# A two-layer block of SSM, attention, FWHT-FFN and MoE on one core: attention's statistics at the start of the second mixture pass, head work one block earlier, another order of the stack writes and loads

## The reference, cut to what matters

```python
# mixture (before and after attention), added with a factor 0.5
scores = sigmoid(xt @ gate_w.T); top-2 of 8 experts, weights scaled by 2.5
h = einsum('td,edh->eth', xt, w1); u = einsum('td,edh->eth', xt, w3)     # H = 176
y = einsum('eth,ehd->etd', silu(h) * u, w2)
routed = einsum('etd,te->td', y, combine); shared = silu(xt @ sw1) * (xt @ sw3) @ sw2
# attention, 16 heads of 16, causal, with ALiBi
q, k, v = proj(Wq, bq), proj(Wk, bk), proj(Wv, bv)
scores = q k^T / sqrt(16), masked above the diagonal, + alibi_bias
out = softmax(scores) @ v, then @ Wo.T + bo
```

## Time and profile before

| | us |
|---|---|
| median of 3 runs | 806.44 |
| lowest and highest | 806.35, 807.98 |
| the profiled execution | 805.94 |
| its span in the trace | 804.1 |

### The profile page before, as it was taken

How to read it: one execution, slowest core, us unless ns; L and a number is a source line. 1 busy time by engine, 2 the same in 40 slices (tenths; PEclk the granted TensorE clock), 3 DMA queues, 4 the chain that set the end, 5 groups by cost and what they waited for, 6 DMA issues and landing times.

```text
span 804.1 us, 10910 instructions
## 1 busy us (share of the span) xinstructions
PE 708.6 (88%) x4054; PEld 485.6 (60%) x4089; DVE 549.1 (68%) x962; ACT 405.6 (50%) x594; POOL 242.8 (30%) x190
## 2 busy tenths in 40 slices
PE   3899998895688799899999999994889998788998
PEld 3587664451234354557877887882447887434787
DVE  4544589999979999974457466366755656944644
ACT  3454597676557688742233344450476442274322
POOL 0001158786429587850996000001000001000000
PEclk9999999997999799999999999998999999899999
DMA  8300012222112221318001000043000043000000
GB/s 290 127 2 0 1 66 78 70 77 66 52 39 68 66 73 61 90 42 243 0 1 23 1 1 1 13 107 104 15 1 1 15 121 99 5 28 1 1 1 26
DMA packets 30609, 41.78 MB, mean 52 GB/s; under 512 B 3769, under 2 KB 19971, under 8 KB 30531
## 3 DMA queue, kind: packets, MB, share of 16 engines
q1 hardware_dynamic: 29306, 40.91, 16.9%
q10 hardware_dynamic: 1252, 0.19, 0.2%
HBM read 36.73 MB, written 4.26 MB: 51 GB/s over the span
## 4 chain that ended last, share of the span: by engine, by line
PE 52%; issue 16%; DVE 15%; ACT 6%; DMA 6%; POOL 3%; SPq 2%; POOLq 0%; DVEq 0%; ACTq 0%
PE PS L500 32%; DVE PS L2066 4%; PE PS L607 3%; DVE shared L2074 3%; PE PS L1095 3%; POOL shared L2390 3%; PE PS L1078 2%; DMA route<-scratch_c 2%; ACT shared L1618 2%; DVE route L2124 1%; PE PS L458 1%; DMA scratch_k<-shared 1%; DMA shared<-in_L_ffn_W_dram 1%; SPq L2336 1%; ACT shared L1544 1%
## 5 line engine op out<-in xcount | busy, mean ns | idle before, releaser
L2390 POOL TENSOR_TENSOR shared<-shared,route 128x1024 f32<-128x1024 f32 x64 | 150.6, 2357 | 72.2 <-DVE shared L2074 67.5
L2074 DVE TENSOR_TENSOR_SCAN shared<-shared,PS 128x512 f32<-128x512 f32 x128 | 148.8, 1204 | 2.4 <-ACT shared L1544 1.7
L500 PE MATMUL PS<-xnT,work_r 128*128 128x512 f32 (+1 forms) x596 | 149.8, 398 | 0.4 <-DVE gated L1798 0.2
L500 PE MATMUL PS<-xnT,weights_r 128*128 128x256 f32 (+1 forms) x732 | 147.1, 349 | 1.4 <-issue 1.1
L500 PEld LDWEIGHTS PS<-xnT,weights_r 128*128 128x128 f32 x732 | 113.5, 191 | 47.3 <-issue 33.4
L500 PEld LDWEIGHTS PS<-xnT,work_r 128*128 128x128 f32 (+1 forms) x596 | 109.2, 188 | 25.0 <-DVE gated L1798 1.7
L1544 ACT ACTIVATE shared<-shared,cols 128x512 f32<-128x512 f32 x128 | 85.2, 715 | 28.3 <-DVE shared L2074 27.8
L500 PE MATMUL PS<-weights_r,work_r 128*128 128x256 f32 (+1 forms) x624 | 89.3, 294 | 0.6 <-DVE gated L1923 0.3
L2066 DVE TENSOR_TENSOR PS<-shared,PS 128x512 f32<-128x512 f32 x128 | 81.3, 681 | 3.5 <-PE PS L940 3.1
L500 PEld LDWEIGHTS PS<-weights_r,work_r 128*128 128x128 f32 (+1 forms) x624 | 80.5, 190 | 2.3 <-issue 0.4
L888 PE MATMUL PS<-shared,cf 64*64 64x512 f32 x512 | 75.0, 658 | 0.6 <-POOL shared L2390 0.6
(11 more groups left out here) (231 smaller groups left out, 1052.4 us busy)
## 6 DMA issues: line engine op xcount, KB each, us to landing
route<-scratch_c SPq DMA_DIRECT2D x64, 256.0 KB, 3.2
shared<-in_L_ffn_W_dram SPq DMA_DIRECT2D x3, 1024.0 KB, 8.7
scratch_k<-shared SPq DMA_DIRECT2D x12, 128.0 KB
scratch_q<-shared SPq DMA_DIRECT2D x12, 128.0 KB
shared<-scratch_k SPq DMA_DIRECT2D x8, 192.0 KB
shared<-scratch_q SPq DMA_DIRECT2D x8, 192.0 KB
mamba_w<-in_L_ffn_w_dram SPq DMA_DIRECT2D x2, 704.0 KB, 5.3
beside<-in_L_ffn_w_dram SPq DMA_DIRECT2D x2, 704.0 KB, 7.7
```

The lines of the kernel that those rows point to most:

```text
L500: last = nc.tensor.matmul(o, lhs[l], rhs[r], start=(start and i == 0), stop=(stop and i == 2))
L2074: v.tensor_tensor_scan(hst[:, (t % 2 * 2 + j) * T:(t % 2 * 2 + j + 1) * T], decay[t % D_SLOTS][:, j * T:(j + 1) * T], products[:, j * T:(j ...
L2390: nc.gpsimd.tensor_tensor(hc[:, u * 2 * T:(u * 2 + n) * T].rearrange("p (c t) -> p c t", c=n), hst[:, (t % 2) * 2 * T:(t % 2 * 2 + n) * T] ...
```

## The change

Three things are edited.

- `LATE_NORM_AT` goes from 4 to 3 and `LATE_HEAD_AT` from 6 to 5. Statistics' square root, scaling, transposes, projections, values and casts of the first batch's attention each come one block earlier.
- DVE's `norm_statistics(0)` is taken out of block `LATE_NORM_AT` and stands at the very beginning of the late pass, ahead of the routing.
- SP's order in `attention_moves`, in both batches, was: six writes of c = 0, fill 1, fill 2, six writes of c = 1, fill 3, fill 4. It is now: six writes of c = 0, four of c = 1 (hi and mid), fill 1, the last two writes of c = 1, fill 2, fill 3, fill 4.

```diff
-LATE_NORM_AT, LATE_HEAD_AT, EARLY_CAST_AT = 4, 6, 4
+LATE_NORM_AT, LATE_HEAD_AT, EARLY_CAST_AT = 3, 5, 4
...
+                if late:
+                    self.norm_statistics(0)
                 if early:
                     self.norm(0, it + 1)
...
-                    if late and p == LATE_NORM_AT:
-                        self.norm_statistics(0)
                     if late and p == LATE_NORM_AT + 1:
                         self.norm_scale(0, 2 * ATTN + 1)
...
-                for c in range(DC):
-                    for quad in (2 * c, 2 * c + 1):
-                        sp.wait_ge(s[f"stacked{quad}"], b * 16 * 6)
-                    for i, part in enumerate(("hi", "mid", "lo")):
-                        for n, parts, scratch, _ in sources:
-                            sp.wait_ge(s["cast"], cast_at(b, c, f"{n}_{part}"))
-                            sp.dma_start(scratch[c, i].rearrange("d h t -> h d t"), part_of(parts, c, i))\
-                                .then_inc(s[f"wrote{n}{c}"], 16)
+                def write(c, i):
+
+                    for n, parts, scratch, _ in sources:
+                        sp.wait_ge(s["cast"], cast_at(b, c, f"{n}_{('hi', 'mid', 'lo')[i]}"))
+                        sp.dma_start(scratch[c, i].rearrange("d h t -> h d t"), part_of(parts, c, i))\
+                            .then_inc(s[f"wrote{n}{c}"], 16)
+
+                def fill(c, quad):
...
+                for quad in range(2 * DC):
+                    sp.wait_ge(s[f"stacked{quad}"], b * 16 * 6)
+                for i in range(3):
+                    write(0, i)
+                for i in range(2):
+                    write(1, i)
+                fill(0, 0)
+                write(1, 2)
+                fill(0, 1)
+                fill(1, 0)
+                fill(1, 1)
```

31 lines of the change are left out of this document (15 added, 16 removed).

## The result

| | before | after |
|---|---|---|
| median, us | 806.50 (4 runs, 806.35 to 807.98) | 799.79 (4 runs, 798.86 to 801.02) |
| ratio | | 0.9914, 95% interval 0.9895 to 0.9932 |
| the profiled execution | 805.94 | 799.49 |
| its span | 804.1 | 797.7 |

The kernel is faster by 6.7 us on the medians and by 6.45 us in the profiled executions. The same kernel was run again beside the experiments; over all its 17 executions the median is 799.28.

The account below looks back on a forecast made before the run. PE's 8.8 us wait for fill 3 before the first attention's `late_unit(0)` was taken as the bound. 805.94 - 5.3 (pass's +1.3 included) + 0.5 + 0.2 = 801.3; the median 0.5 above, 801.8 us, range 800.6 to 804.9.

Parts of the forecast that it names:

- The bound: First attention: PE idle 8.8 us before `late_unit(0)`, waiting for fill 3; DVE is what is late next.
- Part 1: Late pass: head work one block earlier makes the pass end 1.3 us later, casts move 3.2 us earlier.
- Part 2: Start of the late pass: statistics cost DVE 2.1 us, hidden in its 2.54 us wait, so nothing.
- Part 3: First batch, SP's new order: fill 3 lands in time, `late_unit(0)` moves from 562.13 to 556.8, -5.3 us.
- The term behind U: First attention, from `late_unit(0)` on: +0.2 us for the queue and +0.5 us for the clock.
- The queue: `scores(0)` waits for the row of maxima behind fill 4's traffic: +0.2 us (0 to 0.6).
- The clock: First attention after `late_unit(0)` will look like the second, wholly or in part: +0.5 us (0 to 1.0).
- Part 4: Second batch, SP's new order: only the fills move, with cover of 5 and 3 us; costs nothing.
- (a): DMA takes the wait over: a further fill costs 9.5 us, `scores(0)` follows no sooner than 566.3; 804.4 us, chance 0.15.
- (d): Slower: more fills in a row drag on each other (F, time per further fill), both batches; 811.8 us, chance 0.07.
- (b): The clock falls in block 4 of the late pass, 2 us lost; 803.8 us, chance 0.09.
- (e): Better: no clock loss and shorter stalls in block 4, -6 us; 800.4 us, chance 0.05.

Follow-up runs that it names:

- e2: Kernel after with SP's old order, so head work one block earlier and statistics at the start alone; 805.06 us, ratio 0.9978.
- e6: Kernel before with only the statistics moved to the start of the late pass; 806.72 us, ratio 1.0003.
- e15: Kernel before with idle products ahead of `late_unit(0)` (26 in the first attention, nine in the second) and four ahead of `scores(4)`; 804.36 us, ratio 0.9973.
- e5: Kernel after, unchanged, run again; 801.47 us, ratio 0.9933.
- e11: Kernel after, unchanged, run a third time; 798.74 us, ratio 0.9905.
- e10: Kernel after with POOL's add of the output bias started so that it always meets DVE's low parts; 800.57 us, ratio 0.9929.
- e9: Kernel after with POOL's add of the output bias held until DVE has taken four maxima; 800.59 us, ratio 0.9928.
- e14: Kernel after with nine idle products ahead of `late_unit(0)` and four ahead of `scores(4)`, in both attentions; 799.42 us, ratio 0.9909.
- e8: Kernel before with 16-row loads of q, nine idle products ahead of `late_unit(0)` and statistics at the start of the late pass; 796.47 us, ratio 0.9885.
- e4: Kernel after with nine idle products ahead of `late_unit(0)` in both attentions; 799.86 us, ratio 0.9913.
- e7: Kernel before with 16-row loads of q and nine idle products ahead of `late_unit(0)`; 797.04 us, ratio 0.9888.
- e12: e8 with POOL's add of the output bias held until DVE has taken four maxima; 797.83 us, ratio 0.9891.
- e13: e8 with four more idle products ahead of `scores(4)` in each attention; 796.51 us, ratio 0.9877.
- e1: Kernel before with SP's new order alone; 803.55 us, ratio 0.9954.
- e3: Kernel before with each broadcast load of q cut into loads of 16 rows; 799.89 us, ratio 0.9908.

## Why the prediction was off

Point by point, in the order of its steps.

- **The bound** was read right: the wait was for fill 3, fill 3 was late by SP's order and ACT's casts, and taking it away leaves DVE.
- **Part 1** came true almost to the tenth. xn was expected at 492.1, and PE's first transposes are at 492.38 after 1.69 us (1.9 expected); the second at 495.38 after 0.73 (495.2, 0.9). R to Q is 1.32 us longer (+1.3).
- **Part 2** came true: DVE's idle 2.54 us became 0.34.
- **Part 3, the fills.** Fill 1 was issued at 528.59 (528.3). Fill 2 landed 20.8 us later and not 19.0: a pair of writes between two fills costs 2.9 us, not 1.1. PE waited 0.51 us for it, which was to be none, but DVE had no gap. Fill 3 was there in time. U: 556.95 against 556.8.
- **The term behind U is the step that failed.** The prediction put +0.2 for the queue and +0.5 for the clock, neither of which could fall below nothing; the measured stretch is 1.18 us shorter. All of it lies between U and `scores(0)`, 6.33 us before and 5.16 after; from there to O both take 31.9. The two profiles split it.
- *The queue, +0.2 put, -1.04 measured.* In the kernel before, `scores(0)` waited 1.04 us for the row of maxima behind fill 4; after, it doesn't wait. The sum's own figures left room for that: the queue was to end 4.8 to 7.4 us earlier than the 568.46 at which the row landed, and PE's start was to move by 5.3. The experiments bear it out. With SP's old order and broadcast loads the stretch takes 6.31 to 6.40 us in before, e2, e6 and e15, whatever the clock (0.51 in e15, 0.76 in before, and e15 still waits 0.16 us). With the new order and at least a part of it at the full level it takes 4.91 to 5.50.
- *The clock, +0.5 put, -0.13 measured.* Without the wait for the row the stretch takes 5.29 us before and 5.16 after. It was written that the first attention "will now look like the second", and lose clock by it. But the earlier trace rows show the first attention of before at 0.50 up to U and at 0.76 behind it: it was already paying, and with a wait of 2.20 us in place of 8.80 it could as well pay less. The second attention's 0.53 was taken for what a wait of 2.20 us brings; it was one draw of several. Behind the same 2.20 us the kernel after took 37.06, 38.07 and 37.05 us from U to O in three profiles, and 39.16, 37.70 and 37.06 in the second attention.
- So part of the 1.18 us is luck. With the draw of e5 (0.50 all the way, 6.06 us, PE itself being late) the end of the queue brings 0.27 us and no more, and the kernel after would have been 0.9 us longer there, still on the side of a gain. Both are needed for the 1.18: a queue that ends in time, and a clock that doesn't stay at the half level all the way.
- **A term was missing.** The prediction went through PE, DVE, ACT and SP, and not through POOL, whose add was freed 11 us earlier by the new writes. It costs 1.6 to 1.75 us from R to Q in the profiles in which it meets DVE's low parts (e5, e11 and, by force, e10). It was absent from the profiled execution, so it isn't in the 5.27, and it works against the change.
- **Part 4** came true: no wait for a stack in the second attention, and U2 waits 2.20 us for DVE as before.
- **The rivals.** None of (a) to (d) came; for (b), the granted clock was 1.00 from 490 to 500. (e), "no clock loss", had the right sign and 800.4, and its reason was half right; it had a chance of 0.05 and stood outside what the range took in. The range's lower end was the forecast's terms at their best, and no term could be below nothing for the clock. With as much room below nothing as above it (-1.0 to +1.0) it would have begun at 799.6, and held the time. (In (d), the balance of the two attentions turns near F = 10.15 by the prediction's own terms, not 10.3; nothing hangs on it.)

What stays open is the median to less than 1 us. e9 and e10 both lie 1.8 us above e11 and differ from it only in POOL's add, whose place explains neither. The mean granted clock of their executions is 0.9673 and 0.9705, and 0.9730 in e11; by the line in the last section that would be some 2.3 and 1.0 us. It isn't shown whether the hold brings that lower clock or whether it was drawn. And e14, with the half level gone from both attentions, isn't faster by its median than after. The last section shows the draws that such medians of five or six executions carry.

## What to carry to other kernels

A clock, a queue or a wait that the profile shows as already paid is a term that can be given back: ask of each whether it is paid now before adding it to the change's price, and leave it room on both sides of nothing. When a transfer moves up, follow its semaphore to every engine that waits on it, the idle ones too; work that was harmless where it stood can land beside an instruction that it stops. And before work is rearranged around a slow transfer, look at how many DMA engines share it: here 16-row loads alone were worth what the whole change was, and with products that bridge PE's wait and the statistics at the start (e8) the kernel is 1.15% faster than before, more than the change's 0.86%.

## What the runs showed of the hardware

**The same program falls to the half level in one execution and not in the next, and its time follows.** In the 17 executions of the kernel after, the mean granted clock runs from 0.966 to 0.979 and the time from 797.0 to 803.1 us; the eight with 0.974 or more took 797.0 to 799.5, the six below 0.972 799.0 to 803.1. A straight line through them gives 0.4 us for each 0.001 of the clock (correlation -0.71), and the same through 69 executions of the kernel before gives 0.39 (-0.75). The mean clock of these is 0.9647 and of those 0.9722; by that line 2.9 us of the 6.8 between their mean times go with the clock. That is a correlation (a wait can lower the clock and lengthen the time at once), and only the 2.5 us of e15 are shown by an edit.

**The draws come in other stages too.** The profiles of before and of e5 differ in the state-space stage, where all kernels run the same code (columns as in rows 5):

```profile
300.00:320.00 20.00, 18.28 (x111) 10.64 (x112) 18.98 (x23) 15.29 (x23) 15.18 (x8) 1.00 0.20 66
```
```profile
300.00:320.00 20.00, 17.89 (x101) 9.83 (x94) 16.60 (x21) 13.61 (x19) 12.90 (x7) 0.91 0.21 66
```

The first, before, reaches R at 474.56; the second, e5, at 476.79. Seven of the 17 profiles reach it at 476.4 to 476.9. This is why the stretches are counted from R.

**A covered wait leaves the next one.** Products that kept PE busy through the 2.20 us held the clock at the full level there in 13 attentions out of 13 (two each of e4, e7, e8, e12, e13 and e14, one of e15). Behind a later wait of 1.33 us the clock still fell in the second attention of e7, e8 and e12, and 1.5 to 1.6 us went with it; but it fell there too in before, after, e1 and e3, and in the first attention of e9, all without products. Only e13 has a fall that no other profile shows, behind a wait of 1.41 us in the mixture after the second attention (1.4 us). In e4 and e14 there was none. What decides which wait is hit was not settled, and that covering one wait hands the fall to the next isn't shown but perhaps in e13.

**DVE waits for POOL as a whole.** Two instructions of 0.38 us each became 2.5 to 2.95 us beside one add of 2.4 us on POOL.

**Fills in a row.** Two fills of 768 KB each took some 16 us with broadcast loads of q, and 10.5 us in 16-row loads. While q's loads moved, the DMA share was 0.12 to 0.20 before and 0.77 to 0.91 in e3, and the rate 35 to 82 and 205 to 213 GB/s; the loads of k reached 0.87 and 266 GB/s before as well.
